# Graph attention and message passing on one core: the upper clip of the scores moves from a ScalarE pass into VectorE's multiply by the counts

## The chip, the cores and the metric

One core of a Trainium2 chip. The metric is the device time of the whole kernel in microseconds (us). Three executions of the kernel before took 2204.08, 2208.19 and 2205.88 us; the median is 2205.88.

## The reference

There are 3125 nodes of 128 features and 100000 edges (src, dst), sorted by dst in the input. A graph attention layer comes first, then a message network with three dense layers for each edge. What the change touches is in the attention layer:

```
h = x @ kernel
score = leaky_relu(h[src] @ a1 + h[dst] @ a2, 0.2)
e = exp(clip(score, -2, 2))
alpha = e / (segment_sum(e, src) + 1e-7)
out = segment_sum(h[dst] * alpha, src)
x = layernorm(x + out)
```

## The kernel before

The attention works on a dense matrix of nodes by nodes. For each block of 125 nodes (25 blocks, `BLK`) it needs two matrices of 125 x 3125: how often each pair is an edge (`cnt`), and the exponential of the pair's clipped score (`pr`). Their product is the weight by which TensorE sums the rows of h.

**Counts.** A block is made of five windows of 25 nodes (`WPB`, `WIN`), 125 windows in all. A window's counts are a sum of matmuls of one-hot matrices over tiles of 128 edges. The first two tiles of a window (`GATHERED`) have their wide one-hots gathered from HBM by GpSimd (`head_n`, L615), two indirect DMAs a window, into one of three buffers; the third tile's are made by ScalarE in two passes (L730, L735). VectorE makes the narrow one-hots (L849) and all of those for the further tiles, two at a time (`ring_n`, L862). TensorE sums in PSUM (L664, L673, L682). ScalarE copies the window's sum to one of three stage buffers (L760, the eviction), and SyncE writes the stage to `cnt` by two DMAs (L553, L554), which spread 125 x 625 numbers into rows of 3125. `cnt` has two buffers, PSUM two banks.

**Scores.** For block b, ScalarE makes the lower-clipped branch (L770) from the sums of both halves of the score, shifted up by 2. VectorE takes the maximum with the other branch (L829, `leaky`, in parts of 1875 and 1250 columns). ScalarE then makes 4 minus that, held at zero from below (L773, the upper clip), and the exponential of 2 minus that (L741, `exp`). VectorE multiplies by the counts (L839, `weigh`, in the same two parts). `pr` has four slots. TensorE sums over two blocks at a time in nine chunks (L650, `sum_chunk`), and VectorE adds each chunk to `acc` (L820).

**Order.** No planner sets the order: each engine runs the same hand-written loop over blocks v = -1 to 23 and windows u = 0 to 4, and semaphores tie them together. In ScalarE's body each window has `apart_of`, the eviction, and `third_hot`; behind these stand `exp(v)` at u = 0 (`EXP_AT`), the lower clip of the next block at u = 1 (`LOW_AT`), and its upper clip at u = 4 (`CAP_AT`). VectorE has `leaky` behind windows 3 and 4 and `weigh` behind windows 2 and 4 (`LEAKY_AT`, `WEIGH_AT`). The first part of `weigh` waits for Exp and for all the stage writes of its block. TensorE's head matmul of a window waits for its bank (evicted two windows before), for VectorE's narrow one-hots and for the gathers; GpSimd's gathers wait for the head matmul three windows before. The last block's Exp and multiply stand behind the loop.

After the attention comes a barrier, then the message stage, from about 807 us to the end.

The core of the two places:

```
if u == CAP_AT:                                                          # L771
    act.wait_ge(leaky_ready, (t * BPT + v + 2) * 2)
    act.activation(slot, slot, ACT.Relu, bias=caps[:, 0:1], scale=-1.0).then_inc(capped_ready, 1)
dve.tensor_tensor(slot, slot, cnt[0:BLK, v % 2, slice(*PROB_CUTS[part])], ALU.mult).then_inc(prob_ready, 1)   # L839
```

Of the kernel before, what the change touches and what calls it, by code (L numbers as in the profile page):

```python
# [3 lines left out]


P = 128
# [4 lines left out]
NBLK, BLK = 25, 125  # L11
# [28 lines left out]
BPT = 4  # L40
# [6 lines left out]
PROB_CUTS = ((0, PROB_CUT), (PROB_CUT, N))  # L47
# [2 lines left out]
SHIFT_AT = 2  # L50
EXP_AT = 0
LOW_AT = 1
CAP_AT = 4


GT = 4
# [9 lines left out]
EPS_LN = 1e-05  # L66
SLOPE = 0.2
CLIP = 2.0

fp32 = mybir.dt.float32  # L70
f32r = mybir.dt.float32r
# [3 lines left out]
ALU = mybir.AluOpType  # L75
ACT = mybir.ActivationFunctionType
# [21 lines left out]
def index_tables(nc, src, dst, x, w0, att, T, scr_tile, scr_dst, scr_win, scr_pass, scr_eye, table_b):  # L98
# [3 lines left out]
    with ExitStack() as ctx:  # L102
# [250 lines left out]
        def _(act):  # L353
# [16 lines left out]
            for c in range(7):  # L370
                n0, n1 = c * 512, min(N, (c + 1) * 512)
                act.wait_ge(s1_done, c + 1)
                act.activation(T.s1r[:, n0:n1], psT[c % 4][:, 0:n1 - n0], ACT.Copy).then_inc(s1_copied, 1)
            act.activation(T.s2_low[:, :], T.hx[:, 1:NBLK + 1, D + 1], ACT.Copy, bias=CLIP, scale=SLOPE)
            act.activation(T.s2_up[:, :], T.hx[:, 1:NBLK + 1, D + 1], ACT.Copy, bias=CLIP)
            act.activation(T.hx[:, :, D:D + 1], onesf[0:BLK, 0:NBLK + 1].rearrange("p (b o) -> p b o", o=1), ACT.Copy)


def attention(nc, T, scr_eye, wm1, bm1, table_a, table_b):
# [7 lines left out]
    with ExitStack() as ctx:  # L387
        def sb(name, shape, dt):
            return ctx.enter_context(nc.sbuf_tensor(name, shape, dt))

        def sem(name):
            return ctx.enter_context(nc.semaphore(name))
# [5 lines left out]
        cnt = sb("cnt", [P, 2, N], fp32)  # L398
# [7 lines left out]
        ring_n = sb("ring_n", [P, RING, TPT, SWE], bf16)  # L406
        block_keys = sb("block_keys", [P, 2, 2 * KEYS], i16)
        row_at = sb("row_at", [P, ROWS_AT, GATHERED], i32)
        caps = sb("caps", [BLK, 2], fp32)
        stage = sb("stage", [P, STAGES, SWE], fp32)  # L410
        psC = [ctx.enter_context(nc.psum_tensor(f"psC{i}", [P, 2, 512], fp32)) for i in range(2)]
        psO = [ctx.enter_context(nc.psum_tensor(f"psO{i}", [P, 512], fp32)) for i in range(2)]
# [17 lines left out]
        w = cnt[:, 1, NB * 3 * H:NB * 3 * H + 2 * H]  # L430
        b1 = cnt[:, 1, NB * 3 * H + 2 * H:NB * 3 * H + 3 * H]
        cleared = sem("cleared")
        caps_ready = sem("caps_ready")
        head_ready = sem("head_ready")
        head_free = sem("head_free")
        row_ready = sem("row_ready")
# [9 lines left out]
        sp_order = sem("sp_order_a")  # L446
        pool_order = sem("pool_order_a")
        low_ready = sem("low_ready")
        capped_ready = sem("capped_ready")
        leaky_ready = sem("leaky_ready")  # L450
        exp_ready = sem("exp_ready")
        prob_ready = sem("prob_ready")
# [25 lines left out]
        def pair(g):  # L478
            return list(range(2 * g, min(NBLK, 2 * g + 2)))

        def pairs_of(c):

            return [g for g in range(PAIRS) if 0 <= c < CH and pair(g)[-1] // BANK_BLKS == c]

        def some_nodes(c):
            return c * DM, min(WIN, (c + 1) * DM)
# [7 lines left out]
        def blocks(eng, body):  # L494


            for v in range(-1, TURNS_A * BPT):
                body(0, v)
# [222 lines left out]
        @block.scalar  # L721
        def _(act):
            act.sem_inc(bank_read, 2)
            regs = [act.alloc_register(f"act_win{i}") for i in range(WPB)]

            def apart_of(u, made):

                third = act.snap(act.snap(regs[u], min_val=0, max_val=PACK * TILES) >> 10, min_val=0, max_val=TILES - 1) + GATHERED
                act.wait_ge(third_ready, made + 1)
                act.activation(apart[:, :], T.iota_n[:, :], ACT.Square, bias=T.edge_keys[:, 1, bass.ds(third, 1)], scale=-1.0).then_inc(apart_ready, 1)  # L730

            def third_hot(w, made):

                act.wait_ge(apart_ready, made + 1)
                act.activation(third_n[:, w % HEADS, :], apart[:, :], ACT.Relu, bias=1.0, scale=-1.0).then_inc(third_ready, 1)  # L735

            def exp(b):

                slot = pr[:, (b + 1) % PR, :]
                act.wait_ge(capped_ready, b + 1)  # L740
                act.activation(slot, slot, ACT.Exp, bias=caps[:, 1:2], scale=-1.0).then_inc(exp_ready, 1)  # L741

            act.reg_load(regs[0:2], T.win_tab[0:1, 0:2])
            act.sem_inc(third_ready, 1)
            for w in range(2):
                apart_of(w, w)
                third_hot(w, w)

            def body(t, v):
                slot = pr[:, (v + 2) % PR, :]  # L750
                b = t * BPT + v + 1

                made = (v + 1) * WPB + 2
                act.reg_load(regs, T.win_tab[0:1, bass.ds(made, WPB)])
                for u in range(WPB):
                    w = (v + 1) * WPB + u
                    apart_of(u, made + u)
                    act.wait_ge(window_summed, t * (BPT * WPB) + w + 1 + HEADS)
                    act.wait_ge(stage_out[w % STAGES], 32 * (w // STAGES) + 32)
                    act.activation(stage[0:WME, w % STAGES, :].rearrange("p (k n) -> p k n", k=2), psC[w % 2][0:WME, :, 0:HALF], ACT.Copy,  # L760
                                   accum_out=T.edges_of[0:WME, bass.ds(t * (BPT * WPB) + w, 1)]).then_inc(bank_read, 1)
                    third_hot(w + 2, made + u)
                    if u == EXP_AT and v >= 0:
                        exp(v)
                    if u == LOW_AT:
                        if v >= 0:
                            act.wait_ge(chunk_done, t * (2 * CH) + (v // 2) * CH + CH)
                        else:
                            act.wait_ge(caps_ready, 2)
                        act.activation(slot, s1r[0:BLK, :], ACT.Relu, bias=T.s2_low[:, bass.ds(b, 1)], scale=SLOPE).then_inc(low_ready, 1)  # L770
                    if u == CAP_AT:  # L771
                        act.wait_ge(leaky_ready, (t * BPT + v + 2) * 2)
                        act.activation(slot, slot, ACT.Relu, bias=caps[:, 0:1], scale=-1.0).then_inc(capped_ready, 1)  # L773
            blocks(act, body)
            exp(NBLK - 1)
            for c in range(CH + 3):
                if 2 <= c <= DCUTS + 1:
                    a, z = some_nodes(c - 2)
                    act.wait_ge(edges_summed, c - 1)
                    act.activation(T.inv.rearrange("p (w m) -> p m w", m=WIN)[:, a:z, :],  # L780
                                   psD[:, 0:(z - a) * NWIN].rearrange("p (m w) -> p m w", w=NWIN), ACT.Copy).then_inc(edges_read, 1)
                for g in pairs_of(c - 3):
                    s, i = g % NB, len(pair(g))
                    act.wait_ge(rest_ready[1], g + 1)
                    act.activation(b_st[:, s, 0:i, 2, :], rest[:, s, 0:i, :], ACT.Copy).then_inc(part_ready[2], 1)
                if c < CH:
                    bs = slice(chunk(c)[0], chunk(c)[-1] + 1)
                    act.wait_ge(var_ready, c + 1)
                    act.activation(T.std[:, bs], T.den[:, bs], ACT.Sqrt).then_inc(std_ready, 1)
                if 1 <= c <= CH:  # L790
                    a, z = chunk(c - 1)[0] * BLK, (chunk(c - 1)[-1] + 1) * BLK
                    act.wait_ge(x_turned, c)
                    act.activation(T.x1T[:, a:z], psX[:, 0:z - a], ACT.Copy).then_inc(x_copied, 1)
                for g in pairs_of(c - 2):
                    s, i = g % NB, len(pair(g))
                    act.wait_ge(rest_ready[0], g + 1)
                    act.activation(b_st[:, s, 0:i, 1, :], rest[:, s, 0:i, :], ACT.Copy).then_inc(part_ready[1], 1)
                for g in pairs_of(c - 1):
                    s, i = g % NB, len(pair(g))
                    act.wait_ge(ab_done, g + 1)  # L800
                    if g >= NB:
                        act.wait_ge(b_out[s], 32 * (g // NB))
                    act.activation(b_st[:, s, 0:i, 0, :], psC[g % 2][0:BLK, 1, 0:i * H].rearrange("p (b h) -> p b h", h=H), ACT.Copy).then_inc(part_ready[0], 1)

        @block.vector
        def _(dve):
            def step(ins):
                dve.wait_ge(chain.sem, chain.inc(ins))
            dve.memset(caps[:, 0:1], 2.0 * CLIP).then_inc(caps_ready, 1)
            dve.memset(caps[:, 1:2], CLIP).then_inc(caps_ready, 1)  # L810
            dve.sem_inc(chunk_added, len(banks))
            dve.tensor_copy(block_keys[:, 0, :], T.row_keys[:, :, :].rearrange("p c n -> p (c n)")).then_inc(keys_shifted, 1)

# [17 lines left out]
            def weigh(t, v, part):  # L831

                slot = pr[:, (v + 1) % PR, slice(*PROB_CUTS[part])]
                if part == 0:
                    for s in range(STAGES):
                        stored = ((t * BPT + v + 1) * WPB - 1 - s) // STAGES + 1
                        dve.wait_ge(stage_out[s], 32 * stored + 32)
                    dve.wait_ge(exp_ready, t * BPT + v + 1)
                dve.tensor_tensor(slot, slot, cnt[0:BLK, v % 2, slice(*PROB_CUTS[part])], ALU.mult).then_inc(prob_ready, 1)  # L839

            def shift_keys(v):

# [714 lines left out]
```

## Time and profile before

| What | Value |
|---|---|
| Median of three executions | 2205.88 us (2204.08 to 2208.19) |
| Span of the profiled execution | 1891.9 us |
| Median less that span | 314.0 us |
| TensorE busy | 1647.0 us (87%) |
| VectorE busy | 1575.9 us (83%) |
| ScalarE busy | 1335.9 us (71%) |
| GpSimd busy | 1149.9 us (61%) |
| Attention loop within the span | about 94 to 722 us |
| Message stage within the span | about 807 to 1892 us |

The page gives no device time of its own for the profiled execution; its span is the time between its first and last profiled instruction, and the median less the span is what lies around it. Busy times are of an engine's own instructions, without waits. PE is TensorE, PEld its weight loads, DVE is VectorE, ACT is ScalarE, POOL is GpSimd, SP is SyncE. An idle time is the time that the engine stood still just before an instruction, with the one whose end released it behind an arrow. "PEclk" is the granted TensorE clock as a share of 2.4 GHz.

### The profile page before, as it was taken

The page shows a single profiled execution, that of the slowest core. Times are in us where ns is not written, and L with a number is a line of the kernel's source. Part 1 is how long each engine was busy: PE and PEld are TensorE (multiplying, and loading weights), DVE is VectorE, ACT ScalarE, POOL GpSimd, SP SyncE. Part 2 cuts the span into 40 slices and gives each one's busy share as a digit, 9 for nine tenths or more (in the row PEclk, how much of TensorE's full clock was granted, in tenths as well). Part 3 has the DMA queues.
Part 4 walks back from the last instruction along what each step waited for, and adds up shares of the span by engine and source line. Part 5 has one row for each costly group of instructions (what it writes and reads, how often), then busy time and mean ns, then how long its engine had stood idle before and what let it go on. Part 6 is the DMA issues. An engine that isn't in the chain of part 4 may idle for free.

```text
span 1891.9 us, 53764 instructions
## 1 busy us (share of the span) xinstructions
PE 1647.0 (87%) x15240; PEld 1425.0 (75%) x15240; DVE 1575.9 (83%) x3400; ACT 1335.9 (71%) x2302; POOL 1149.9 (61%) x1202
## 2 busy tenths in 40 slices
PE   5767888887786776669999999999999999999986
PEld 3445677766575655459999999999999999999964
DVE  5778999887667766769999999999999999999986
ACT  5024678888888873557777777777777777777751
POOL 4212456666665651257777777777777777777720
PEclk9899999998888786979999999999999999999999
DMA  4023467788878871555555554555445555544411
GB/s 100 21 50 71 105 130 144 142 146 148 145 145 137 143 136 34 164 140 142 140 141 140 141 143 140 140 141 141 139 141 142 141 140 142 142 140 141 140 49 34
DMA packets 141999, 236.59 MB, mean 125 GB/s; under 512 B 27997, under 2 KB 92849, under 8 KB 141914
## 3 DMA queue, kind: packets, MB, share of 16 engines
q0 software_dynamic: 49632, 142.89, 31.2%
q1 hardware_dynamic: 92282, 92.71, 21.4%
q8 instruction: 35, 0.57, 0.2%
q14 instruction: 50, 0.41, 0.1%
HBM read 185.78 MB, written 10.66 MB: 104 GB/s over the span
## 4 chain that ended last, share of the span: by engine, by line
PE 55%; DVE 1%; DMA 0%; ACT 0%; issue 0%; POOL 0%; SPq 0%; ACTq 0%; DVEq 0%; POOLq 0%
PE ps L1271 11%; PE ps L1272 10%; PE ps L1277 10%; PE ps L1251 9%; PE psA L1289 6%; PE ps L1246 5%; PE ps L1256 2%; PE ps L990 1%; PE ps L1001 1%; PE ps L998 1%; PE psA L1009 0%; DMA bias_f<-in_L_gnn_bm 0%; DVE x L1062 0%; DMA ga<-table_a,idx 0%; ACT u L1023 0%
## 5 line engine op out<-in xcount | busy, mean ns | idle before, releaser
L1222 POOL DMA_INDIRECT ga<-table_a,idx x784 | 761.4, 971 | 248.0 <-issue 226.4
L615 POOL DMA_INDIRECT head_n<-scr_eye,row_at x250 | 305.1, 1221 | 311.7 <-PE psC L664 209.6
L1271 PE MATMUL ps<-wm_hi,h_hi 128*128 128x256 f32 x1568 | 402.9, 292 | 0.7 <-ACT h_hi L1323 0.7
L1272 PE MATMUL ps<-wm_lo,h_hi 128*128 128x256 f32 x1568 | 381.8, 278 | 0.0
L1327 ACT ACTIVATE h<-ps 128x512 bf16<-128x512 f32 x392 | 234.0, 597 | 177.0 <-PE ps L1277 176.8
L1271 PEld LDWEIGHTS ps<-wm_hi,h_hi 128*128 128x128 f32 x1568 | 294.9, 188 | 30.8 <-ACT h_hi L1323 27.1
L1425 DVE TENSOR_TENSOR h<-rest,h 128x512 bf16<-128x512 f32 x392 | 269.2, 687 | 53.0 <-ACT h L1331 53.0
L1420 DVE SCALAR_TENSOR_TENSOR rest<-ps,h 128x512 f32<-128x512 f32 x392 | 268.0, 687 | 33.2 <-ACT h L1327 16.3
L1272 PEld LDWEIGHTS ps<-wm_lo,h_hi 128*128 128x128 f32 x1568 | 295.5, 188 | 0.0
L673 PE MATMUL psC<-ring_n,ring_m 128*126 x1180 | 235.8, 331 | 56.7 <-DVE ring_n L862 30.1
L1414 DVE SCALAR_TENSOR_TENSOR h_lo<-ps,h_hi 128x512 fp32r<-128x512 f32 x392 | 264.3, 691 | 11.1 <-ACT h_hi L1323 4.6
L1323 ACT ACTIVATE h_hi<-ps 128x512 fp32r<-128x512 f32 x392 | 234.1, 597 | 43.1 <-PE ps L1251 23.8
L673 PEld LDWEIGHTS psC<-ring_n,ring_m 128*126 x1180 | 167.5, 146 | 108.8 <-issue 99.8
L1277 PE MATMUL ps<-wm_hi,h_lo 128*128 128x256 f32 x1568 | 245.2, 278 | 0.0
L1331 ACT ACTIVATE h<-rest 128x512 bf16<-128x512 f32 x392 | 243.3, 621 | 0.0
L1251 PE MATMUL ps<-ident,ga 128*128 128x128 f32 x1568 | 237.7, 273 | 1.4 <-DMA ga<-table_a,idx 1.4
L1251 PEld LDWEIGHTS ps<-ident,ga 128*128 128x128 f32 x1568 | 198.2, 141 | 34.7 <-DMA ga<-table_a,idx 2.7
L760 ACT ACTIVATE stage<-psC 126x626 f32<-126x626 f32 x125 | 85.6, 685 | 196.0 <-PE psC L682 193.7
L862 DVE TENSOR_SCALAR ring_n<-iota_n,edge_keys 128x626 int16 x590 | 212.2, 401 | 0.0
L1277 PEld LDWEIGHTS ps<-wm_hi,h_lo 128*128 128x128 f32 x1568 | 210.1, 188 | 0.0
L664 PE MATMUL psC<-head_n,head_m 128*126 128x313 bf16 x500 | 109.9, 337 | 89.3 <-DMA head_n<-scr_eye,row_at 62.8
L839 DVE TENSOR_TENSOR pr<-pr,cnt 125x1875 f32<-125x1875 f32 (+1 forms) x50 | 90.3, 1808 | 89.5 <-DMA cnt<-stage 58.1
(193 smaller groups left out, 2657.6 us busy)
## 6 DMA issues: line engine op xcount, KB each, us to landing
dstb<-scr_dst SPq DMA_DIRECT2D x196, 126.0 KB
cnt<-stage SPq DMA_DIRECT2D x125, 195.3 KB
cnt<-stage SPq DMA_DIRECT2D x125, 109.9 KB
ga<-table_a,idx POOLq DMA_INDIRECT x784, 2.9
bw<-table_b SPq DMA_DIRECT2D x196, 63.0 KB
table_b<-cnt SPq DMA_DIRECT2D x12, 336.0 KB
head_n<-scr_eye,row_at POOLq DMA_INDIRECT x250
table_a<-pr SPq DMA_DIRECT2D x12, 224.0 KB
```

Of the source, the lines that this page charges most:

```text
L615: pool.indirect_dma_start(head_n[:, w % HEADS, s, :], None, scr_eye, bass.IndirectOffsetOnAxis(ap=row_at[:, w % ROWS_AT, s:s + 1], axis=0) ...
L673: last = pe.matmul(bank[0:WME, k, 0:HALF], ring_m[:, bass.ds(slot, 1), :, s].rearrange("p o m -> p (o m)"), ring_n[:, bass.ds(slot, 1), s, ...
L1222: pool.indirect_dma_start(ga[:, u, k, :], None, table_a, bass.IndirectOffsetOnAxis(ap=idx[:, u, k:k + 1], axis=0)).then_inc(gathered[u][k] ...
L1251: last = pe.matmul(bank[:, t * P:(t + 1) * P], ga[:, s, t, k * P:(k + 1) * P], T.ident[:, :], is_transpose=True, start=False, stop=True, s ...
L1271: pe.matmul(ps2[q][:, t % 2, :], hi, w_hi[:, k, :], start=False, stop=True, skip_group_check=True)
L1272: pe.matmul(ps2[q][:, t % 2, :], hi, w_lo[:, k, :], start=False, stop=True, skip_group_check=True)
L1277: last = pe.matmul(ps2[q][:, t % 2, :], h1_lo[:, u % 2, k, t * P:(t + 1) * P], w_hi[:, k, :], start=False, stop=True, skip_group_check=True)
L1323: act.activation(h1_hi[:, u % 2, k, :], ps1[u % 2][k][:, :], ACT.Relu).then_inc(hi_ready, 1)
L1331: act.activation(h2[1][:, u % 2, 2 * q:2 * q + 2, :], rest1[:, u % 2, 2 * q:2 * q + 2, :], ACT.Copy).then_inc(part2_ready, 1)
L1414: dve.scalar_tensor_tensor(h1_lo[:, u % 2, k, :], ps1[u % 2][k][:, :], 0.0, h1_hi[:, u % 2, k, :].bitcast(fp32), ALU.max, ALU.subtract).th ...
L1420: dve.scalar_tensor_tensor(rest1[:, u % 2, 2 * q:2 * q + 2, :], ps2[q][:, :, :], 0.0, h2[0][:, u % 2, 2 * q:2 * q + 2, :], ALU.max, ALU.su ...
L1425: dve.tensor_tensor(h2[2][:, u % 2, 2 * q:2 * q + 2, :], rest1[:, u % 2, 2 * q:2 * q + 2, :], h2[1][:, u % 2, 2 * q:2 * q + 2, :], ALU.sub ...
```

## The change

The upper clip's pass on ScalarE (L771 to L773), its constant and its semaphore go. Exp is taken of the shifted score minus 2, waits for the two parts of `leaky`, and is not clipped from above. VectorE's multiply by the counts becomes one instruction that first takes the minimum with e squared and then multiplies.

```diff
-CAP_AT = 4
+CEIL = math.exp(CLIP)
...
-        caps = sb("caps", [BLK, 2], fp32)
+        centre = sb("centre", [BLK, 1], fp32)
...
-                act.wait_ge(capped_ready, b + 1)
-                act.activation(slot, slot, ACT.Exp, bias=caps[:, 1:2], scale=-1.0).then_inc(exp_ready, 1)
+                act.wait_ge(leaky_ready, (b + 1) * 2)
+                act.activation(slot, slot, ACT.Exp, bias=centre[:, 0:1]).then_inc(exp_ready, 1)
...
-                            act.wait_ge(caps_ready, 2)
+                            act.wait_ge(centre_ready, 1)
...
-                    if u == CAP_AT:
-                        act.wait_ge(leaky_ready, (t * BPT + v + 2) * 2)
-                        act.activation(slot, slot, ACT.Relu, bias=caps[:, 0:1], scale=-1.0).then_inc(capped_ready, 1)
...
-            dve.memset(caps[:, 0:1], 2.0 * CLIP).then_inc(caps_ready, 1)
-            dve.memset(caps[:, 1:2], CLIP).then_inc(caps_ready, 1)
+            dve.memset(centre[:, :], -CLIP).then_inc(centre_ready, 1)
...
-                dve.tensor_tensor(slot, slot, cnt[0:BLK, v % 2, slice(*PROB_CUTS[part])], ALU.mult).then_inc(prob_ready, 1)
+                dve.scalar_tensor_tensor(slot, slot, CEIL, cnt[0:BLK, v % 2, slice(*PROB_CUTS[part])], ALU.min, ALU.mult).then_inc(prob_ready, 1)
```

## Rows read from the trace of the kernel before

**Rows 1.** The page: busy shares, and ScalarE's busy tenths in 40 slices.
```profile
PE 1647.0 (87%) x15240; PEld 1425.0 (75%) x15240; DVE 1575.9 (83%) x3400; ACT 1335.9 (71%) x2302; POOL 1149.9 (61%) x1202
...
ACT  5024678888888873557777777777777777777751
```

**Rows 2.** Windows view: stretch, its length, busy us by engine, clock, DMA.
```profile
90.00:150.00 60.00, 41.19 (x216) 29.22 (x214) 45.13 (x143) 13.58 (x21) 9.95 (x17) 0.97 0.21 42
...
200.00:250.00 50.00, 41.32 (x270) 33.57 (x270) 47.46 (x124) 32.92 (x42) 25.22 (x26) 1.00 0.51 111
...
300.00:350.00 50.00, 42.28 (x290) 36.66 (x289) 43.57 (x96) 44.77 (x53) 32.73 (x34) 0.97 0.83 143
...
650.00:700.00 50.00, 34.92 (x210) 27.93 (x208) 31.88 (x60) 42.91 (x52) 32.16 (x33) 0.84 0.83 145
...
250.00:700.00 450.00, 350.92 (x2203) 293.41 (x2201) 351.43 (x736) 381.21 (x466) 284.47 (x303) 0.88 0.80 143
```

**Rows 3.** Group of the evictions, ScalarE, 94 to 250 us: busy, mean, idle before.
```profile
L760 ACT ACTIVATE stage<-psC 126x626 f32<-126x626 f32 x20 | 13.8, 691 | 128.8 <-PE psC L682 128.8
```

**Rows 4.** ScalarE, 250 to 700 us: groups, and its wait (total, times, longest).
```profile
L760 ACT ACTIVATE stage<-psC 126x626 f32<-126x626 f32 x101 | 69.0, 684 | 60.6 <-PE psC L682 58.2 <-DMA cnt<-stage 2.1
...
L773 ACT ACTIVATE pr<-pr,caps 125x3125 f32<-125x3125 f32 x20 | 57.8, 2888 | 0.0
...
ACT stage L760 <- PE psC L682: 58.2, 43, 3.9
```

**Rows 5.** Waits of TensorE and GpSimd, 250 to 700 us: total, times, longest.
```profile
PE psC L664 <- DMA head_n<-scr_eye,row_at: 52.7, 38, 3.8
...
PE psC L664 <- ACT stage L760: 2.7, 2, 1.8
...
POOL head_n L615 <- PE psC L664: 83.6, 47, 4.1
```

**Rows 6.** DMA view, 250 to 700 us: GB/s in 40 slices; queues' share.
```profile
GB/s 139 113 147 134 137 141 163 132 149 146 150 135 147 145 148 142 127 159 154 160 131 152 141 153 110 163 161 149 143 126 127 148 139 139 141 154 143 161 143 125
...
q0 software_dynamic: 9679, 32.33, 40.9%
q1 hardware_dynamic: 15066, 31.39, 38.8%
```

**Rows 7.** Timeline at four block boundaries: last matmul, eviction of window 0 (start, duration).
```profile
449.14 0.51 PE L682 MATMUL psC<-third_n,head_m 128*126 128x313 bf16 x2
...
451.08 0.68 ACT L760 ACTIVATE stage<-psC 126x626 f32<-126x626 f32 x1
...
491.43 0.51 PE L682 MATMUL psC<-third_n,head_m 128*126 128x313 bf16 x2
...
495.15 0.68 ACT L760 ACTIVATE stage<-psC 126x626 f32<-126x626 f32 x1
...
607.76 0.69 ACT L760 ACTIVATE stage<-psC 126x626 f32<-126x626 f32 x1 [2.75 <-PE psC L682]
...
670.85 0.73 PE L682 MATMUL psC<-third_n,head_m 128*126 128x313 bf16 x2
...
672.38 0.68 ACT L760 ACTIVATE stage<-psC 126x626 f32<-126x626 f32 x1
```

**Rows 8.** Groups by form, VectorE, 250 to 700 us: multiply and leaky step.
```profile
L839 DVE TENSOR_TENSOR pr<-pr,cnt 125x1875 f32<-125x1875 f32 x21 | 44.4, 2112 | 85.2 <-DMA cnt<-stage 58.1 <-ACT pr L741 27.1
L829 DVE SCALAR_TENSOR_TENSOR pr<-x1T,s_up,pr 125x1875 f32<-125x1875 f32 x20 | 43.3, 2167 | 7.8 <-ACT pr L770 7.6
```

**Rows 9.** Timeline of the loop's tail, and the multiply's durations (min/median/max).
```profile
718.21 5.43 POOL L626 TENSOR_TENSOR pr<-node_inv,ident 25x3125 f32<-25x3125 f32 x1 [13.72 <-DVE node_inv L885]
719.12 2.90 ACT L741 ACTIVATE pr<-pr,caps 125x3125 f32<-125x3125 f32 x1
...
722.15 4.82 DVE L839 TENSOR_TENSOR pr<-pr,cnt 125x1875 f32<-125x1875 f32 x2 [4.10 <-ACT pr L741]
...
L839 DVE TENSOR_TENSOR pr<-pr,cnt x50: 1444/1779/3453, 170.1 to 725.5; 125x1875 f32<-125x1875 f32 x25, 125x1250 f32<-125x1250 f32 x25
```

More of the change, by code:

```diff
@@ L3 @@
 from contextlib import ExitStack
+import math
 P = 128
@@ L432, in attention @@
         cleared = sem("cleared")
-        caps_ready = sem("caps_ready")
+        centre_ready = sem("centre_ready")
         head_ready = sem("head_ready")
@@ L448, in attention @@
         low_ready = sem("low_ready")
-        capped_ready = sem("capped_ready")
         leaky_ready = sem("leaky_ready")
```

## The prediction

> **What bounds the kernel now.** I began with the page's busy shares [rows 1]. TensorE leads over the whole span (87%), but that is an average over two stages. ScalarE's slices show them: its load is 8 of ten in slices 7 to 14, which lie in the attention loop, and a flat 7 in the long message stage behind. The change touches the loop alone, and everything behind the loop follows a barrier, so what the loop loses or gains is carried to the end one to one. All of the working below is therefore about the loop, about 94 to 722 us of the span.
>
> The stretches [rows 2] cut the loop in two. Up to about 250 us ScalarE is busy 14 of 60 us and then 33 of 50 us, while VectorE is at 45 of 60 and 47 of 50: VectorE builds many one-hot tiles for the crowded low nodes, and ScalarE waits. Before the 20 evictions of that part, four blocks, ScalarE sits idle 128.8 us in all [rows 3], so the four clips there lie in idle time. From 250 to 700 us (101 windows, so 20 of the 25 blocks, at about 22 us each) ScalarE is the busiest engine, with 381.2 of 450 us (85%); TensorE and VectorE have 351 each (78%). At first sight that is a kernel bound by ScalarE, and the change takes work from just that engine.
>
> The waits say otherwise. In the late stretch ScalarE still idles 58.2 us before its evictions, waiting for TensorE's last matmul of the window (43 of 101 windows) [rows 4]. TensorE in its turn idles 52.7 us before the head matmuls of 38 windows until a gathered one-hot row block arrives from HBM, and only 2.7 us, in two windows, until an eviction of ScalarE [rows 5]. The gathers are issued by GpSimd, which itself waits 83.6 us for TensorE to give a head buffer free, because there are three of them. That is a ring: head matmul, gather issue, landing, head matmul three windows on. ScalarE is not in it. The DMA engines carry two streams in that stretch, the gathers (40.9% of the engines) and the writes of the counts (38.8%), at 143 GB/s on average against 163 in the best slice [rows 6]: they are nearly full as well. So the late stretch has three limits close together: ScalarE's 85%, the DMA's 80%, and the ring of gathers that pays the DMA's queueing.
>
> **The change part by part.**
>
> Removed: 25 clips of 2.888 us on ScalarE, 72.2 us of work. Four lie in the early idle time and give nothing [rows 3], the 20 of the late stretch are 57.8 us [rows 4], and one is in the tail. The other three ScalarE passes of the loop are untouched, and Exp costs the same with another bias and scale.
>
> What the clip delays: it stands after the eviction of a block's window 4, so the first thing behind it that others wait for is the eviction of window 0 of the next block. TensorE's head matmul two windows on, the stage write, and then Exp all follow that eviction. I compared the eviction's start with the end of TensorE's last matmul of the window at every block boundary. Where the eviction starts with a wait on TensorE, the clip was hidden, as at 607.76, with 2.75 us of idle behind the clip and the pass after it. Where it starts later than the matmul's end (plus the 0.05 us that the hidden cases show), ScalarE was late, as at 451.08 (1.4 us late), 495.15 (3.2) and 672.38 (0.7) [rows 7]. Ignoring delays of 0.1 us, 9 of the 25 boundaries are late, the first and last at 451 and 672, and they add up to 11.9 us. At these, the clip's removal moves the window's release forward by the delay and no further, since TensorE is then the later one. That is my first-order gain, **11.9 us**.
>
> Second order: time given back at one boundary makes ScalarE less late at windows 1 and 2, behind Exp and the lower clip, and a smoother eviction lets TensorE idle less, so some more can follow; against that the DMA has only 12% of room (143 against 163) and TensorE is already waiting for gathers. I add 2 us, an estimate from these two, and keep 0 and the full bound for the range.
>
> Exp comes 2.9 us earlier behind each boundary. The multiply by the counts waits for Exp and for the block's stage writes; of its 85.2 us of late idle, 58.1 end with a stage write and 27.1 with Exp [rows 8]. The writes are not moved by the clip, except as the first-order gain already counts. I count nothing more.
>
> Added: the multiply becomes a scalar-tensor-tensor, with one more arithmetic stage in the same pass over the same 1875 or 1250 columns. The trace has the new form in the leaky step, on float32 in SBUF of the same shape: 2167 ns against 2112 for the old one [rows 8]. At 0.055 us for each of the 50, VectorE works 2.8 us more. The leaky step reads its scalar from memory and the new one has a constant, so the difference could also be nothing; 0 and 2.8 are the two ends. VectorE idles 85.2 us before the 1875-column multiply, but those waits precede the instruction and the added time follows it. I take a quarter on the path, **0.7 us**, since VectorE is one of four engines in that ring.
>
> Removed waits: ScalarE's wait for the leaky step moves from window 4 to Exp in window 0 of the next block. It is later in order and so easier. No DMA is added or moved; SyncE and GpSimd queues are as before. The shorter constant fill and the one semaphore less are nothing.
>
> The tail: after the last block the clip and Exp (719.12) run one behind the other, and VectorE's last multiply starts at 722.15 when Exp ends. The removal would let it start 2.9 us earlier. But GpSimd runs a product of 3125 columns from 718.21 to 723.64, and the multiply, beside it for 1.5 us, took up to 3453 ns where its like takes 2112 [rows 9]: it lost 1.34 of the 1.49 us of overlap. Started at 719.3 it would overlap for 4.3 us and, at that rate, end within 0.4 us of where it ends now. The last stage write also has to land. I take **0.4 us** of gain; the ends are 0 and 2.9. The Trainium skill has a rule that speaks against this gain (SBUF — State Buffer, "Who interferes with whom"): a VectorE instruction with two SBUF inputs contends with a GpSimd instruction that reads SBUF. By that rule the tail gives about nothing, and without it 2.9 us. The 3453 ns agree with it.
>
> Sum: 11.9 + 2 - 0.7 + 0.4 = 13.6 us, rounded to 13. The profiled span is 1891.9 us; it would become 1879. The median shown, 2205.9, is 314.0 us longer than the span; what lies around the span is not touched, so the median becomes **2193**.
>
> **The rivals.**
>
> ScalarE is the real limit (gain over 25 us). For: 85% busy, and it was late at 58 of the 101 late windows by the waits' count. Its lateness at windows 1 and 2 could be the same delay passed along. The granted clock also speaks for it: in 300 to 350 us it is 0.97 of 2.4 GHz, with TensorE busy 42 of 50 us, and 0.84 in 650 to 700 with 35 of 50 [rows 2], so a denser TensorE may see less of 1.2 GHz. The ceiling is the 57.8 us removed, or by the DMA 450 x (1 - 143/163) = 55 us if its best slice held throughout, which it does not. 25 to 45 us gives 2161 to 2181. Against: TensorE's idle time ends with gathers.
>
> The ring of gathers and the DMA take it all (gain within 4.4 us). Every microsecond that ScalarE gives is then waited for the next gather. For: TensorE's 52.7 us behind gathers against 2.7 behind evictions [rows 5]. What remains is the tail less the added VectorE time, from +0.7 to -3: 2203 to 2206.
>
> Slower: the writes come in the gathers' way. Without the clip, two ScalarE passes instead of three follow one another, the evictions at the boundary come closer together, and with them the stage writes. If each of the waits on gathers (38 in the waits' view, 52.7 us) grew by 0.34 us, it would cost 13 us and wipe out the gain; that is the point from which it decides. At 0.6 us it costs 23 against 13: 2216. For: the DMA's slices already range from 110 to 163 GB/s, which is bursty. Against: no byte is added and the evictions' order stays. The Trainium skill states (DMA: Bandwidth & Descriptors, "Issuing engines are not separate DMA queues") that transfers from different issuing engines run on the same 16 engines and interleave; a rule under which the two streams could hurt each other this way.
>
> The change doesn't do what it says: a clip inside the multiply could cost a second pass. Then 50 x 1.8 us more on VectorE would show at once. The leaky row, two operations in one pass at 2167 ns, all but excludes it; I put it with the slower case.
>
> **How the numbers follow.** About 0.2% (4.4 us) is what a measurement of this kernel can tell from no change. Forecast, a gain of 5 to 25 us: 0.50. ScalarE the limit, over 25: 0.17. Absorbed, within 4.4: 0.20. Slower by more than 4.4: 0.13. So faster 0.67, same 0.20, slower 0.13. The range runs from 2168 (a gain of 38, most of the second case) to 2209 (the absorbed case, the full 2.8 us of VectorE and a trace of the slower one).
>
> **What would show it.** The clip's line is gone and ScalarE's busy time in the loop falls by 72 us. The late blocks take about 21.5 us each rather than a little over 22. The eviction of window 0 starts with a wait on TensorE at almost every boundary, and ScalarE's idle time before evictions grows by about 45 us: removed work that becomes waiting. TensorE's waits on gathers stay or grow. The multiply takes 2.17 us, and the last one is stretched by GpSimd's product. I am wrong if late blocks fall below 20.9 us, if the waits on gathers shrink, if the multiply takes over 2.3 us, or if the gather waits grow by more than 13 us.

## The result and the profile after

The changed kernel took 2201.0 us (median of 20 executions, 2190.24 to 2323.72) against 2204.65 us (2197.66 to 2213.53, 20 executions) for the kernel before. The ratio is 0.9973, with a 95% interval of 0.996 to 0.9986: 6.0 us faster, from 3.1 to 8.8. The execution of 2323.72 us ran at a granted clock of 0.65, where all the others had 0.94 or more, and does not count in the ratio. The two medians as they stand differ by 3.7 us, so the size is known to a few microseconds only. The kernel is faster, as forecast, and the time lies in the range; the size is a little under half of the 13 us that I forecast.

The page of the changed kernel, the rows that answer to [rows 1]:

```profile
span 2200.1 us, 53738 instructions
...
PE 1730.4 (79%) x15240; PEld 1461.3 (66%) x15240; DVE 1602.2 (73%) x3399; ACT 1268.4 (58%) x2277; POOL 1152.5 (52%) x1202
...
ACT  4034677777777435665565665665565566655651
```

ScalarE is down by 67.5 us and 25 instructions. The span, though, is 308 us longer than before, and the profiled execution took 2201.89 us, so only 1.8 us lie around it. That difference lies in the message stage (1085 us before, 1403 after), which the change does not touch, and goes with the chip. It has a part of its own at the end. The loop can be compared.

Block by block, by the start of the eviction of window 0 in the timelines of both kernels (first three lines before, then three after; blocks 4, 12 and 24):

```profile
250.24 0.68 ACT L760 ACTIVATE stage<-psC 126x626 f32<-126x626 f32 x1
...
426.43 0.69 ACT L760 ACTIVATE stage<-psC 126x626 f32<-126x626 f32 x1
...
693.79 0.69 ACT L760 ACTIVATE stage<-psC 126x626 f32<-126x626 f32 x1 [2.44 <-PE psC L682]
```

```profile
248.69 0.69 ACT L760 ACTIVATE stage<-psC 126x626 f32<-126x626 f32 x1 [2.17 <-PE psC L682]
...
425.07 0.69 ACT L760 ACTIVATE stage<-psC 126x626 f32<-126x626 f32 x1 [2.01 <-issue]
...
689.16 0.69 ACT L760 ACTIVATE stage<-psC 126x626 f32<-126x626 f32 x1 [1.46 <-issue]
```

Blocks 4 to 11 took 176.2 us before and 176.4 after. Blocks 12 to 23 took 267.4 and 264.1. From the first eviction to the last the loop is 7.7 us shorter; the rest of it lies in the first four blocks (1.1) and in the last block (3.6, where the cut kernels below show 0.4). So eight of the twenty blocks that I had counted as open to a gain gave none. The windows view of just those eight blocks, before and then after, and TensorE's wait on gathers in them before:

```profile
250.00:426.00 176.00, 146.77 (x976) 124.47 (x975) 159.73 (x367) 150.56 (x185) 106.36 (x119) 0.96 0.77 142
```

```profile
249.00:425.00 176.00, 146.94 (x975) 125.10 (x975) 159.71 (x366) 128.95 (x176) 106.36 (x118) 0.95 0.79 142
```

```profile
PE psC L664 <- DMA head_n<-scr_eye,row_at: 1.1, 1, 1.1
```

ScalarE lost 21.6 of 150.6 us, and no other engine's busy time moved by more than 0.7. VectorE is busy 159.7 of 176 us (91%) there, 9 us more than ScalarE even before. The gathers are not what TensorE waits for: of the 52.7 us of [rows 5], these eight blocks hold 1.1. So VectorE is the likeliest limit there; no run tested it.

ScalarE's group of evictions in 250 to 700 us, the waits in the same stretch, and VectorE's two steps, answering to [rows 4], [rows 5] and [rows 8]:

```profile
L760 ACT ACTIVATE stage<-psC 126x626 f32<-126x626 f32 x102 | 70.1, 687 | 105.2 <-PE psC L682 78.0 <-issue 25.0 <-DMA cnt<-stage 2.1
...
PE psC L664 <- DMA head_n<-scr_eye,row_at: 51.2, 38, 3.4
PE psC L664 <- ACT stage L760: 3.0, 3, 1.2
...
POOL head_n L615 <- PE psC L664: 83.5, 47, 4.5
...
L825 DVE SCALAR_TENSOR_TENSOR pr<-x1T,s_up,pr 125x1875 f32<-125x1875 f32 x21 | 45.5, 2165 | 10.3 <-ACT pr L770 9.8 <-issue 0.5
L835 DVE SCALAR_TENSOR_TENSOR pr<-pr,cnt 125x1875 f32<-125x1875 f32 x21 | 44.4, 2113 | 82.2 <-DMA cnt<-stage 68.4 <-ACT pr L741 8.2 <-issue 5.6
```

This is where the work went. ScalarE's idle time before evictions rose from 60.6 to 105.2 us: of the 57.8 us taken out of the stretch, 44.6 came back as waiting. TensorE's waits on gathers did not shrink (52.7 to 51.2), nor did GpSimd's waits on TensorE (83.6 to 83.5) or all of its idle time before gathers (162.5 to 163.2). The multiply waits 8.2 us for Exp where it waited 27.1, and 68.4 for stage writes where it waited 58.1, so most of its relief was handed from one releaser to the other. The multiply's new form takes 2113 ns, the old one took 2112; the leaky step beside it still takes 2165.

The tail, VectorE's and GpSimd's lines, answering to [rows 9], and the first matmul behind it, which stood at 725.66 before:

```profile
706.68 0.69 ACT L760 ACTIVATE stage<-psC 126x626 f32<-126x626 f32 x1 [1.16 <-PE psC L682]
...
710.39 5.43 POOL L626 TENSOR_TENSOR pr<-node_inv,ident 25x3125 f32<-25x3125 f32 x1 [11.76 <-DVE node_inv L881]
...
713.25 5.91 DVE L835 SCALAR_TENSOR_TENSOR pr<-pr,cnt 125x1875 f32<-125x1875 f32 x2 [3.02 <-DMA cnt<-stage]
...
717.84 1.01 PE L650 MATMUL psO<-hx_inv,pr 125*125 125x129 f32 x3 [9.39 <-DVE pr L835]
```

From the last eviction to that matmul it takes 11.2 us; before, the last eviction began at 714.91, and it took 10.8. The clip's 2.9 us are gone from the tail and nothing came of them: the multiply waits until the last stage write lands, and then runs beside GpSimd's product. Its two parts take 5.9 us, of which the first 4534 ns.

### The profile page after: what moved, and what is told of

It is laid out like the page before. It is cut to its first block, busy times and chain, and to the rows that moved or that the text cites. A ratio compares the mean times of both kernels' runs of the same rounds, so it can differ in the third digit from the quotient of the medians.

```text
span 2200.1 us, 53738 instructions
## 1 busy us (share of the span) xinstructions
PE 1730.4 (79%) x15240; PEld 1461.3 (66%) x15240; DVE 1602.2 (73%) x3399; ACT 1268.4 (58%) x2277; POOL 1152.5 (52%) x1202
## 3 DMA queue, kind: packets, MB, share of 16 engines
q1 hardware_dynamic: 92282, 92.71, 18.3%
## 4 chain that ended last, share of the span: by engine, by line
PE 50%; issue 10%; another core or an unknown queue 2%; ACT 1%; DVE 1%; DMA 0%; ACTq 0%; SPq 0%; DVEq 0%
PE ps L1267 11%; PE ps L1273 10%; PE ps L1268 9%; PE ps L1247 8%; PE psA L1285 5%; PE ps L1242 4%; PE ps L1252 2%; PE ps L986 1%; PE ps L997 0%; PE ps L994 0%; ACT h_hi L1319 0%; PE psA L1005 0%; DVE x L1058 0%; DMA bias_f<-in_L_gnn_bm 0%
## 5 line engine op out<-in xcount | busy, mean ns | idle before, releaser
L1267 PE MATMUL ps<-wm_hi,h_hi 128*128 128x256 f32 x1568 | 422.2, 300 | 105.2 <-issue 87.5
L1268 PE MATMUL ps<-wm_lo,h_hi 128*128 128x256 f32 x1568 | 396.9, 285 | 45.2 <-issue 44.7
L1267 PEld LDWEIGHTS ps<-wm_hi,h_hi 128*128 128x128 f32 x1568 | 300.6, 192 | 167.7 <-issue 132.0
L1268 PEld LDWEIGHTS ps<-wm_lo,h_hi 128*128 128x128 f32 x1568 | 301.5, 192 | 73.8 <-issue 73.4
L1273 PE MATMUL ps<-wm_hi,h_lo 128*128 128x256 f32 x1568 | 279.8, 285 | 70.5 <-issue 67.9
L1273 PEld LDWEIGHTS ps<-wm_hi,h_lo 128*128 128x128 f32 x1568 | 222.7, 192 | 59.2 <-issue 58.1
L1285 PE MATMUL psA<-hot_e,h 128*128 128x42 bf16 x4704 | 150.5, 181 | 6.6 <-issue 3.8
```

Source lines behind the costliest of these rows:

```text
L1267: pe.matmul(ps2[q][:, t % 2, :], hi, w_hi[:, k, :], start=False, stop=True, skip_group_check=True)
L1268: pe.matmul(ps2[q][:, t % 2, :], hi, w_lo[:, k, :], start=False, stop=True, skip_group_check=True)
L1273: last = pe.matmul(ps2[q][:, t % 2, :], h1_lo[:, u % 2, k, t * P:(t + 1) * P], w_hi[:, k, :], start=False, stop=True, skip_group_check=True)
L1285: last = pe.matmul(bank[:, k, :], h2[c][:, u % 2, t, k * P:(k + 1) * P], hot_e[:, u % GUN, t, :], start=(t == 0 and c == 0 and k == 0), st ...
```

## The experiments

The full kernel varies by 16 us between executions, so most experiments use a cut form: the message stage is left out, and the first layer's normalised rows are stored instead. The cut kernels ran on three chips: those down to the minimum with ScalarE's clip kept on one, those from the doubled pass to the four head buffers on another, the rest on a third. On the first two the whole kernel before takes 1890.8 and 1891.7 us; the third is compared with them further down. A block's times come from the one profiled execution of a run, which need not be the median one.

```diff
...
-        messages(nc, T, wm2, bm2, table_a, table_b, scr_dst, bm3, wm3, bn1, wn1, wn2, bn2, out)
+            sp.dma_start(out.rearrange("(b n) f -> n b f", b=NBLK)[p0:p1, :, :], T.x1[p0:p1, :, :]).then_inc(stored, 16)
...
```

**The cut kernel before.**

> The kernel before with the message stage left out: behind the attention only the normalised rows are stored (the output is then the first layer's). It is the base for the kernels of the same cut. In the full kernel's profile the attention ended by 807 us, so about 810 to 820 us, and a spread of a few us at most between executions, if the full kernel's spread of 16 us comes mostly from the message stage. The loop, first to last eviction, takes about 621 us as in the profile before.

810.7 us (806.08 to 813.08). The size is as expected. The spread of 7 us is not: the attention alone varies by about half of what the full kernel does. In the profiled execution, of 813.08 us, blocks 4 to 11 took 177.2 us and blocks 12 to 23 270.8.

**The cut changed kernel.**

> The changed kernel, cut in the same way (message stage left out). Theory 1 (gathers and DMA take most of what ScalarE gives): 5 to 9 us less than the cut kernel before, like the full kernel's measured gain of about 6 and the 7.8 us by which the loop is shorter in the two profiles. Theory 2 (the full kernel's gain is small because the message stage hides or gives back part of it): 13 us or more less in the cut kernel.

802.86 us (799.66 to 811.0), 7.8 below by the medians and 5.4 by the means, with ranges that overlap. Blocks 4 to 11: 176.3; blocks 12 to 23: 260.5 (profiled execution 801.11). That fits theory 1, and there is no sign that the message stage hides a gain.

**No upper clip at all.**

```diff
-                dve.scalar_tensor_tensor(slot, slot, CEIL, cnt[0:BLK, v % 2, slice(*PROB_CUTS[part])], ALU.min, ALU.mult).then_inc(prob_ready, 1)
+                dve.tensor_tensor(slot, slot, cnt[0:BLK, v % 2, slice(*PROB_CUTS[part])], ALU.mult).then_inc(prob_ready, 1)
```

> The cut changed kernel with the minimum left out of the multiply: a plain tensor-tensor multiply, so scores are not clipped from above at all. If the added arithmetic stage costs nothing (the profile after has 2113 ns against 2112): within 1 us of the cut changed kernel. If it costs what I predicted, 0.055 us each and a quarter on the path: 0.7 us less, up to 2.8 us less.

806.75 us (795.4 to 812.41), a wider spread than the expected difference; blocks 12 to 23 took 261.9 us against 260.5 (profiled execution 807.88). No sign that the minimum costs anything, and by itself too noisy to exclude 2 us.

**The minimum in the multiply, with ScalarE's clip kept.**

```diff
-                dve.tensor_tensor(slot, slot, cnt[0:BLK, v % 2, slice(*PROB_CUTS[part])], ALU.mult).then_inc(prob_ready, 1)
+                dve.scalar_tensor_tensor(slot, slot, 7.38905609893065, cnt[0:BLK, v % 2, slice(*PROB_CUTS[part])], ALU.min, ALU.mult).then_inc(prob_ready, 1)
```

> The cut kernel before with ScalarE's clip kept and the minimum in the multiply added (one part of the change alone). If the multiply's new form is free: within 1 us of the cut kernel before. If it costs time on the path: 0.7 to 2.8 us more. All of the change's gain then belongs to the removed pass.

809.59 us (804.92 to 812.74), 1.1 below the cut kernel before. With the durations in the profile (2113 against 2112 ns) the added stage is free, and the gain is the removed pass's. Blocks 12 to 23 took 265.4 us here and 270.8 in the cut kernel before, with the same work on ScalarE: a single profile of that stretch is good to some 5 us.

**The clip's pass twice.**

```diff
+        once_ready = sem("once_ready")
...
-                        act.activation(slot, slot, ACT.Relu, bias=caps[:, 0:1], scale=-1.0).then_inc(capped_ready, 1)
+                        act.activation(slot, slot, ACT.Relu, bias=caps[:, 0:1], scale=-1.0).then_inc(once_ready, 1)
+                        act.wait_ge(once_ready, t * BPT + v + 2)
+                        act.activation(slot, slot, ACT.Relu).then_inc(capped_ready, 1)
```

> The cut kernel before (message stage left out) with the upper clip's pass done twice on ScalarE (the second is a Relu that changes nothing), 2.9 us more for each of 25 blocks. Theory 1 (ScalarE is just below the limit in the late blocks, and gathers and DMA set the pace): not the mirror image of the removal; ScalarE would need 439 of the 450 us that the late blocks take, so the slack of 60 us is used up and the time grows by 20 to 45 us, against 5 to 8 us gained by the removal. Theory 2 (each ScalarE microsecond in the late blocks counts): 58 us more. Theory 3 (ScalarE is not in the path at all): under 8 us more.

830.68 us (825.94 to 838.38): 20 us more for 72 us of added work, where removing 72 gained 7.8. The profile is of the longest execution of each of the two kernels, 838.38 and 813.08 us. Blocks 12 to 23 took 14.1 us more there, the first four 4.6, and blocks 4 to 11 186.2 us, 9.0 more; these last are the blocks in which the removal gave nothing. In 420 to 660 us:

```profile
420.00:660.00 240.00, 175.91 (x1030) 147.39 (x1030) 158.75 (x311) 219.05 (x243) 146.04 (x154) 0.82 0.79 136
```

ScalarE is busy 219 of 240 us, against 200 in the cut kernel before. So ScalarE stood just below the pace before: a step up meets it, a step down gives little.

**Half the stage writes, with and without the clip.** Counts are left out; the DMA load falls by a quarter in bytes.

```diff
-                    sp.dma_start(cnt[u * WIN:u * WIN + ROWS_A, (v + 1) % 2, :], stage[0:ROWS_A * SBLK, w % STAGES, 0:SW]).then_inc(stage_out[w % STAGES], 16)
+                    sp.dma_start(cnt[u * WIN:u * WIN + 8, (v + 1) % 2, :], stage[0:8 * SBLK, w % STAGES, 0:SW]).then_inc(stage_out[w % STAGES], 16)
-                    sp.dma_start(cnt[u * WIN + ROWS_A:(u + 1) * WIN, (v + 1) % 2, :], stage[ROWS_A * SBLK:WM, w % STAGES, 0:SW]).then_inc(stage_out[w % STAGES], 16)
+                    sp.dma_start(cnt[u * WIN + ROWS_A:u * WIN + ROWS_A + 4, (v + 1) % 2, :], stage[ROWS_A * SBLK:(ROWS_A + 4) * SBLK, w % STAGES, 0:SW]).then_inc(stage_out[w % STAGES], 16)
...
+                pool.memset(cnt[:, :, :], 0.0).then_inc(cleared, 1)
```

> The cut kernel before with each stage write halved: 40 and 20 of the 80 and 45 stage rows are written, and the counts' buffers are cleared once at the start by GpSimd (so most counts are left out; about 10 us of GpSimd may show early). The DMA then moves about 2.4 MB a block instead of 3.2. Theory 1 (DMA and the ring of gathers set the pace): late blocks shorter by 1 us or more each, 20 us less or more over the loop. Theory 2 (ScalarE sets the pace): late blocks within 0.3 us of before.

788.71 us (783.96 to 791.72): 22 below the cut kernel before, in spite of a start that is 5.7 us later. Blocks 12 to 23 fell from 270.8 to 240.0 us. The DMA's load does set part of the late blocks' pace.

> The same halved writes in the cut changed kernel. Theory 1: with the DMA relieved the removed clip is worth more than the 5 us it gave in the cut kernels: 20 us or more below the halved kernel with the clip, since ScalarE is the limit there. If the clip's removal is small for another reason than the DMA: again about 5 us.

791.65 us (789.12 to 793.13): 3 above the halved kernel with the clip, not 20 below it. Both theories missed. With the DMA half idle, ScalarE fell from 222 to 191 of 240 us busy, and blocks 12 to 23 went from 240.0 to 244.0. So there is a limit beside the DMA and ScalarE. These are the cut changed kernel with halved writes in 420 to 660 us: the stretch, and GpSimd's waits.

```profile
420.00:660.00 240.00, 193.53 (x1202) 160.95 (x1201) 186.59 (x361) 190.60 (x258) 169.71 (x178) 0.87 0.52 117
...
POOL head_n L616 <- POOL row_at L601: 36.8, 45, 0.8
POOL head_n L616 <- issue: 18.3, 60, 0.3
POOL head_n L616 <- PE psC L665: 15.4, 14, 3.5
```

GpSimd is busy 169.7 us, waits 36.8 for its own copy of the row indices, made just before each gather, and 18.3 between instructions: 225 of 240 us are its own. In the halved kernel with the clip the same sum is 230 (170.4, 40.1 and 19.8), so GpSimd was all but full there already, and the clip's removal had little to give.

**Four head buffers instead of three**, full writes. `HEADS` also sets the number of buffers of the narrow one-hots and of the third tile.

```diff
-HEADS = 3
+HEADS = 4
```

> The cut changed kernel with four head buffers instead of three, so the gathers of a window may be issued one window earlier, and the loop's other buffers of that depth (narrow one-hots, third tile) too. Same bytes. If the ring's latency (head matmul, issue, landing) is what TensorE waits for: TensorE's waits on gathers fall from about 50 us to under 20, and the time falls by 8 us or more. If it is the DMA's throughput: the waits move elsewhere and the time falls by under 4 us.

799.51 us (791.96 to 802.57), 3.4 below the cut changed kernel, with ranges that overlap. TensorE's waits on gathers fell to 11.0 us in 250 to 670 us, from 41.6, but its waits on the narrow one-hots rose from 2.1 to 19.4 and those named "issue" from 14.6 to 31.3; before the head matmuls it waited 63.9 us in all with three buffers and 62.5 with four. ScalarE's waits on stage writes rose to 19.8. The waits moved, as for the throughput case; the DMA's share rose from 0.83 to 0.88 in 420 to 660 us.

**Row indices copied two windows ahead.**

```diff
-ROWS_AT = HEADS + 1
+ROWS_AT = HEADS + 2
...
-                    rows_of(w + 1, u + 1)
+                    rows_of(w + 2, u + 2)
```

> The same, with the stage writes halved (so most counts are left out), where the DMA is only half busy and yet the removed clip gave nothing (792 against 789 us). Theory A: GpSimd is the limit there, so the late blocks fall from 20.3 us to 18.5 or less, and the time by 15 us or more. Theory B': a slower TensorE clock (0.85 to 0.87 against 0.91 in the late blocks) holds them at 20: the time falls by under 5 us.

769.95 us (768.54 to 772.29), 22 below the same kernel without it. Blocks 12 to 23: 226.1 us, 18.8 each. The copy's waits fell to 2.9 us, and GpSimd is busy 192 of 240 us. With the DMA relieved, GpSimd's serial issue was the limit. This run and those below were made on a chip on which the kernel before takes 2190 us, where it takes 1891 on those of the other cut runs; the attention seems not to depend on it, since blocks 12 to 23 of the changed kernel took 260.4 us there and 260.5 here.

> The cut changed kernel (message stage left out) in which GpSimd copies a window's row indices two windows ahead instead of one, so that a gather no longer waits 0.82 us for the copy made just before it (41 such waits, 33.6 us, in 420 to 660 us of the cut changed kernel). Bytes and every other engine's work are the same. Theory A (with the clip gone, GpSimd's serial issue of the gathers is the next limit of the late blocks: there it is busy or waiting for itself 217 of 240 us): 8 us or more less than the cut changed kernel's 803 us. Theory B (the DMA's throughput alone is the limit): within 3 us.

With full writes: 805.51 us (804.83 to 811.82), no gain over 802.86. The 33.6 us of waits on the copy fell to 2.2, and GpSimd's idle time named "issue" rose from 17.4 to 77.4:

```profile
420.00:660.00 240.00, 186.24 (x1146) 155.94 (x1147) 172.18 (x336) 181.02 (x246) 158.17 (x166) 0.86 0.87 147
...
POOL head_n L616 <- issue: 77.4, 95, 5.5
POOL head_n L616 <- POOL row_at L600: 2.2, 14, 0.2
```

The gathers could be issued earlier and the blocks were no shorter in the medians: theory B. The DMA moved 147 GB/s as before, at 0.87 of its time against 0.83.

What GpSimd waits for in those 77 us the profile does not name, but its times show it. These are TensorE's head matmul and the gather behind the longest such wait:

```profile
519.29 0.79 PE L665 MATMUL psC<-head_n,head_m 128*126 128x313 bf16 x2 [3.24 <-DMA head_n<-scr_eye,row_at]
...
520.86 0.96 POOL L616 DMA_INDIRECT head_n<-scr_eye,row_at  x1 [5.52 <-issue]
```

The gather starts 0.78 us after the matmul's end. So do 22 of the 25 waits named "issue" that are longer than half a microsecond, 53.5 us together, and so do those named after TensorE in the cut changed kernel (13 of 15). GpSimd waits for a head buffer, TensorE frees it only after a gather has landed, and the time that the copy took has become waiting in that ring: for a free buffer GpSimd waited 24.2 us in the cut changed kernel and about 56 here.

**The full kernels once more.**

> The changed kernel, whole, on the chip on which the kernel before takes about 1891 us (on the chips of the first comparison both took 2200). If the gain lies in the attention alone: 4 to 8 us below the kernel before here too, and the message stage takes about 1085 us as in the profile before, not 1390 as in the profile after, since it belongs to the chip and not to the change.

2183.82 us (12 executions) against 2190.22 (23 executions), ratio 0.998 (0.9962 to 0.9999). The first half of the expectation holds at its lower end: about 4.4 us. The second could not be tried: this chip was not one that runs the kernel before in 1891 us, and the message stage took about 1382 us, against 1403 in the profile after.

> The changed kernel, whole, with four head buffers and the row indices copied two windows ahead. Four head buffers alone took the cut kernel from 803 to 799 us. If both reliefs add: 15 us or more below the kernel before; if the DMA takes the rest: 8 to 12 us below it.

2189.27 us against 2190.22, ratio 1.0008 (0.9982 to 1.0034). The reliefs do not add, and the gain of the changed kernel is not there either. Blocks 12 to 23 took 262.3 us, with the DMA at 0.87 of its time in 420 to 660 us: with both reliefs in place the DMA is the likeliest limit that is left. No whole kernel here beats the changed one; four head buffers alone, 3.4 us better in the cut form and within its spread, were not tried in the whole kernel.

## Why the prediction was right in direction and too large

- **Where ScalarE has room** ([rows 2], [rows 3]). The first four blocks gave nothing to speak of, as predicted (1.1 us in the full profiles, -1.1 in the cut ones), and the hidden part was wider than that: I drew the line at 250 us and took the whole of 250 to 700 us as one stretch. Its mean of 78% for VectorE hid 91% in the first eight blocks, and its 52.7 us of waits on gathers hid that all but 1.1 of them come later. Those 8 of 20 blocks gave 0.
- **The first-order gain of 11.9 us.** All nine late boundaries at which I counted it lie from block 13 on, so that count was not in the wrong blocks. The delay at window 0 did go: over all boundaries ScalarE is late by 1.1 us in the trace after, at two of them. The failing step is "the clip's removal moves the window's release forward by the delay and no further": it took each released microsecond as one of the block's. The next head matmul needs the gather too, and the waits on gathers stayed at 51 us. Blocks 12 to 23 gained 3.3 us in the two full profiles and 10.3 in the two cut ones. Over the three profiles with the pass and full writes (267.4, 270.8, 265.4) and three without it (264.1, 260.5 and 260.4 in the repeated full kernel) they gained 6.2, and blocks 4 to 11 0.4. So of the 10.8 us of delay that went away at window 0 about 6 became time. The other windows make the step look worse still: by the same count over 250 to 700 us, evictions started late at 54 windows before, 76.8 us in all, and at 33 after, 41.7 us. ScalarE's lateness fell by 35 us and the loop by 7.7. My second-order 2 us had no ground.
- **Work that becomes waiting.** "ScalarE's idle time before evictions grows by about 45 us" was met by 44.6. I had this number and the waits on gathers, and should have believed them rather than the delays at the boundaries.
- **The multiply, 0.7 us.** It is 0. The leaky step's 55 ns are not those of a second operation; that step differs in reading its scalar from memory, which may be their cause and was not tried alone.
- **The tail, 0.4 us.** It is 0 (10.8 to 11.2 us). The multiply took 3453 ns beside 1.5 us of GpSimd's product before and 4534 beside 2.6 us of it after, from 2112 elsewhere. The rule of the Trainium skill that the prediction cites (SBUF — State Buffer, "Who interferes with whom"), that a VectorE instruction with two SBUF inputs contends with a GpSimd instruction that reads SBUF, agrees with both traces.
- **"What lies around the span is not touched".** The 314 us were not around the span. The profile of before came from a chip on which the kernel takes about 1892 us, the median from others. It did not harm the sum, since all of its terms were inside the loop.
- **The rivals.** "ScalarE is the real limit" falls by the result itself, 6 us for 57.8 taken out, and by the experiment that halves the writes: with the DMA half idle ScalarE was busy 93% and its clip was still worth nothing. Nor did the clock bear it out: in 650 to 700 us TensorE is busy 41.2 us of 50 after the change, 34.9 before, and the granted clock is 0.84 in both. "The ring and the DMA take it all" was nearest, with 6 us rather than up to 4.4, and the interval from 3.1 to 8.8 does not part it from the forecast; that the gain came out above 5 is partly luck. That GpSimd's own issue time is a wall just behind the DMA was in none of the cases. "The writes come in the gathers' way" did not occur: the waits on gathers did not grow.

What stays open: in 420 to 660 us of the cut kernel before, the DMA at 0.84, ScalarE at 83% and GpSimd's own time at 78% (90% in the changed one) lie close together, and how much of the 6 us each passes on was not separated. The halved kernel without the clip was even 3 us slower than the one with it; GpSimd's issue was full in both, but the granted clock was 0.87 against 0.91, and which follows from which was not tried.

## What to carry to other kernels

Cut a loop into stretches by what each block contains before reading an engine's share: an engine at 85% on average set the pace in no stretch that was looked at. Work taken from an engine outside the ring that sets the pace comes back as its idle time, and the waits of the other engines tell so in advance: if their waits don't name the engine, discount the gain, even where it looks late. When several limits lie within a few per cent of each other, removing one uncovers the next, and doubling the suspected cost measures only how near it is. When a releaser has no name in the profile, compare the start with other engines' ends: a constant distance points to it.

## What the runs showed of the hardware

GpSimd's instruction that issues a gather took 0.96 us (median of 151 in 100 to 700 us of the kernel before) where no multiply or leaky step of VectorE (1.4 to 2.2 us each) ran beside it, never more than 1.6, and up to 2.85 us where one did (median 1.62 of 87):

```profile
411.55 2.11 DVE L839 TENSOR_TENSOR pr<-pr,cnt 125x1875 f32<-125x1875 f32 x1 [3.01 <-ACT pr L741]
411.63 2.85 POOL L615 DMA_INDIRECT head_n<-scr_eye,row_at  x1 [0.30 <-issue]
```

So part of GpSimd's busy time in the late blocks is time lost beside VectorE's multiply and leaky step, which the busy shares do not show. How much a shorter VectorE step would give back was not tried.

The same kernel before took 1891 us on some chips and 2190 to 2205 on others, with the same instructions. The attention takes the same time on both. In the message stage the windows view has, in 1000 to 1500 us, before and then after:

```profile
1000.00:1500.00 500.00, 500.00 (x5786) 459.74 (x5785) 456.45 (x883) 395.99 (x786) 380.38 (x392) 1.00 0.51 141
```

```profile
1000.00:1500.00 500.00, 409.56 (x4360) 364.45 (x4359) 354.87 (x666) 298.60 (x593) 288.09 (x297) 0.98 0.38 107
...
L1267 PE MATMUL ps<-wm_hi,h_hi 128*128 128x256 f32 x590 | 159.6, 301 | 39.4 <-issue 31.3 <-ACT h_hi L1319 7.8
L1273 PE MATMUL ps<-wm_hi,h_lo 128*128 128x256 f32 x590 | 107.2, 287 | 35.9 <-issue 35.1
```

TensorE does 5786 matmuls on the one and 4360 on the other in the same 500 us. On the slower it stands idle between matmuls for reasons the profile does not name ("issue"), at a granted clock of 0.98 of 2.4 GHz. The kernel before was not profiled on a slower chip, but its times there are as long as the changed kernel's, and the change does not touch this stage. The cause was not looked for. It means that a profile and a median can come from different chips, and that the median less the span should be checked before it is taken for time around the span.
